# Projecting a batch's attention values in the last slots of the stage ahead, and holding them in a PSUM bank

## What is computed

```python
Q = (decoder_input @ W_q).reshape(B, Sd, HEADS, HEAD_DIM)
K = (encoder_output @ W_k).reshape(B, Se, HEADS, HEAD_DIM)
V = (encoder_output @ W_v).reshape(B, Se, HEADS, HEAD_DIM)
scores = jnp.einsum('bqhd,bkhd->bhqk', Q, K) / jnp.sqrt(jnp.float32(HEAD_DIM))
attn = jax.nn.softmax(scores, axis=-1)
out = jnp.einsum('bhqk,bkhd->bqhd', attn, V).reshape(B, Sd, E)
return out @ W_o + b_o
```

## Time and profile before

| | |
|---|---|
| median of 3 runs | 523.68 us (523.23 to 525.01) |
| the profiled execution's own time | 522.92 us |
| span in the trace | 519.5 us |
| granted TensorE clock, mean over the span | 0.963 |
| TensorE (PE) busy | 449.5 us, 87% |
| VectorE (DVE) busy | 385.5 us, 74% |
| ScalarE (ACT) busy | 291.4 us, 56% |
| GpSimd (POOL) busy | 214.4 us, 41% |

### The profile page before, as it was taken

The page is one execution under the profiler, slowest core; times in us unless marked ns, Lnnn a source line. Parts: engine busy times, 40 slices in busy tenths (PEclk is TensorE's granted clock), DMA queues, the critical chain, the costliest instruction groups (busy, mean ns, idle before and its releaser), DMA issues.

```text
span 519.5 us, 6244 instructions
## 1 busy us (share of the span) xinstructions
PE 449.5 (87%) x1923; PEld 190.0 (37%) x1923; DVE 385.5 (74%) x642; ACT 291.4 (56%) x516; POOL 214.4 (41%) x213
## 2 busy tenths in 40 slices
PE   8999779889798879899889969998979887878984
PEld 3433434224232213353342314443424332324563
DVE  5889987775779896576897896798647779732285
ACT  3244451552657753845877744646786545697434
POOL 5559795730348983421579771422000011000000
PEclk9999998999979988999999999998989989998998
DMA  6656482512695504134934213220242310000011
GB/s 217 233 152 172 114 215 78 118 37 61 182 231 138 130 1 112 26 77 132 239 96 113 63 29 84 73 72 2 63 110 62 72 52 2 2 0 1 2 40 40
DMA packets 26511, 47.31 MB, mean 91 GB/s; under 512 B 5456, under 2 KB 16368, under 8 KB 26480
## 3 DMA queue, kind: packets, MB, share of 16 engines
q1 hardware_dynamic: 24512, 44.05, 32.1%
q10 hardware_dynamic: 1968, 2.88, 2.1%
HBM read 35.19 MB, written 9.96 MB: 87 GB/s over the span
## 4 chain that ended last, share of the span: by engine, by line
PE 29%; DVE 18%; ACT 6%; issue 4%; DMA 1%; SPq 1%; ACTq 0%; POOL 0%; DVEq 0%
PE bank L665 9%; DVE MX L1615 7%; PE bank L651 6%; PE bank L726 5%; PE bank L712 4%; PE bank L703 3%; DVE W L1532 2%; ACT PT L1223 2%; PE bank L942 1%; DVE st L1498 1%; DVE OT L1625 1%; DMA x1T<-OT 1%; SPq L486 1%; PE bank L972 1%; DVE den L1621 1%
## 5 line engine op out<-in xcount | busy, mean ns | idle before, releaser
L1615 DVE TENSOR_REDUCE MX<-bank 128x1 f32<-128x512 f32 x256 | 165.9, 681 | 82.7 <-PE bank L703 78.3
L1223 ACT ACTIVATE PT<-bank 128x512 f32<-128x512 f32 x256 | 146.2, 597 | 112.9 <-PE bank L712 108.8
L703 PE MATMUL bank<-KS,QS 96*128 96x512 bf16 x240 | 91.6, 398 | 25.0 <-DVE MX L1615 24.3
L712 PE MATMUL bank<-QS,KS 99*128 99x512 bf16 x256 | 97.2, 393 | 12.3 <-ACT PT L1223 9.8
L726 PE MATMUL bank<-PT,Vs 128*32 128x512 f32 x512 | 72.6, 640 | 6.0 <-ACT PT L1223 4.3
L1917 POOL TENSOR_TENSOR W<-qT,W 128x512 f32<-128x512 f32 x48 | 63.1, 1319 | 29.0 <-DVE W L1532 17.2
L712 PEld LDWEIGHTS bank<-QS,KS 99*128 99x128 bf16 x256 | 24.2, 99 | 102.6 <-issue 59.0
L703 PEld LDWEIGHTS bank<-KS,QS 96*128 96x128 bf16 x240 | 23.7, 99 | 71.8 <-DVE MX L1615 45.5
L1948 POOL TENSOR_TENSOR MP<-MX,zero 128x16 bf16<-128x16 f32 x15 | 3.6, 240 | 107.1 <-DVE MX L1615 72.9
L1903 POOL TENSOR_TENSOR W<-kT,W 128x512 f32<-128x512 f32 x32 | 43.3, 1355 | 6.7 <-ACT kT L1074 6.7
L1532 DVE TENSOR_TENSOR_SCAN W<-bank,W 128x512 f32<-128x512 f32 x32 | 38.7, 1210 | 0.0
(11 more groups left out here) (218 smaller groups left out, 710.7 us busy)
## 6 DMA issues: line engine op xcount, KB each, us to landing
W<-v_rows SPq DMA_DIRECT2D x20, 512.0 KB, 9.2
k_parts<-parts SPq DMA_DIRECT2D x24, 128.0 KB, 2.4
KS<-k_parts SPq DMA_DIRECT2D x16, 192.0 KB, 3.7
q_parts<-parts SPq DMA_DIRECT2D x24, 128.0 KB, 2.4
QS<-q_parts SPq DMA_DIRECT2D x16, 192.0 KB, 3.6
cT<-in_cT SPq DMA_DIRECT2D x4, 512.0 KB, 3.4
xtok<-in_x SPq DMA_DIRECT2D x4, 512.0 KB, 10.1
W<-v_rows ACTq DMA_DIRECT2D x4, 512.0 KB, 5.8
```

The lines of the kernel that those rows point to most:

```text
L703: pe.matmul(bank(n, b)[:, :], QS[0:NS, h, i * P:(i + 1) * P], KS[0:NS, h, :], start=True, stop=True).then_inc(filled(n, b), 1)
L712: pe.matmul(bank(name, b)[:, :], KS[0:NR, h, kt * P:(kt + 1) * P], QS[0:NR, h, :], start=True, stop=True).then_inc(filled(name, b), 1)
L1223: act.activation(PT[:, n % 2, j, :], bank(name, b)[:, :], ACT.Exp).then_inc(emptied(name, b), 1)
L1615: dve.tensor_reduce(MX[:, NT * h + i:NT * h + i + 1], bank(n, b)[:, :], AX.X, ALU.max).then_inc(emptied(n, b), 1)
```

## The change

V1 of a batch moves to quarter (14, 1) of the stage ahead of its own and stays in bank 1 until ScalarE reads it, at the same place as before. V0 stays in its own stage for batches 1 and 2, but goes from (0, 0) to (0, 1); for the last batch it moves to (13, 1) of the stage ahead, in bank 2. To have the banks free, the maxima tiles give up bank 1 in quarters 61 to 63 of stages 0 and 1 and bank 2 from quarter 52 of stage 2 on, and mr0 is no longer in bank 1 but takes the least recently used of the maxima banks, as mr3 did already.

```diff
 SIDE_USES = {
-    (0, 0): ("V0", "b", 2), (0, 1): ("V1", "b", 1), (1, 2): ...
+    (0, 1): ("V0", "b", 2), (14, 1): ("V1", "o", 1), (1, 2): ...
...
+THIRD_USES = {**SIDE_USES, (13, 1): ("V0", "o", 2)}
+FOURTH_USES = {at: use for at, use in SIDE_USES.items() if use[0] != "V0"}
...
-    if s == 0 and (46 <= quarter <= 56 or quarter > 60) or s == 1 and (54 <= quarter <= 56 or quarter > 60):
+    if s == 0 and 46 <= quarter <= 56 or s == 1 and 54 <= quarter <= 56:
         spare.append(1)
...
-    if s == 2 and quarter >= 28 or s == 3 and (13 <= quarter <= 21 or 26 <= quarter):
+    if s == 2 and 28 <= quarter <= 51 or s == 3 and (13 <= quarter <= 21 or 26 <= quarter):
         spare.append(2)
...
 def row_bank(s, g):
-    return (1, 0, 1 if s >= 2 else 0)[g]
+    return 0 if g == 1 or s < 2 else 1
...
-                side = SIDE_USES if s else FIRST_USES
+                side = (FIRST_USES, SIDE_USES, THIRD_USES, FOURTH_USES)[min(s, 3)]
...
-                    use(f"mr{g}", stage[which], oldest(max_banks(s, NT * n + i)) if g == 3 else row_bank(s, g))
+                    use(f"mr{g}", stage[which], oldest(max_banks(s, NT * n + i)) if g in (0, 3) else row_bank(s, g))
...
                 if o is not None and b:
+                    sp.wait_ge(*full_of("V0", b))
                     sp.wait_ge(*full_of("V1", b))
                     sp.dma_start(cT[:, :, :], t["cT"][o]).then_inc(cT_in, 16)
...
-                        if b and n == 0 and i < 2:
-                            by_token(f"V{i}", b, cT, xwv, i)
+                        if b and b < LAST and (n, i) == (0, 1):
+                            by_token("V0", b, cT, xwv, 0)
+                        if o == LAST and (n, i) == (13, 1):
+                            by_token("V0", o, cT, xwv, 0)
+                        if o is not None and (n, i) == (14, 1):
+                            by_token("V1", o, cT, xwv, 1)
```

## The result

The changed kernel took 528.84 us (median of 4 runs) against 523.45 us (4 runs) before: ratio 1.0128, 95% interval 1.0075 to 1.0181. In a later session of 12 runs of it and 23 of the kernel before it came to 1.0066 (1.0021 to 1.0111). I had forecast 524.8 us, in a range of 520.8 to 527.4, and no measurable change as the likeliest outcome. The loss is 3.5 to 6.7 us.

The account below looks back on a forecast made before the run. It took VectorE to bound the ends of stages 0 and 1, TensorE the stretch after the boundary and stage 2's end. -0.4 - 1.35 + 1.4 + 1.4 (clock) = +1.05, say +1.1, giving a 524.8 us median, range 520.8 to 527.4.

Parts of the forecast that it names:

- The walk at the full clock: Tile-by-tile timing of stages 0 to 2 with fixed spacings: -0.4, -1.35 and +1.4 us.
- forecast 2.6: Ends of stages 0 and 1: m5.0 waits 2.6 us for m4.3's bank, with value row 14 behind it.
- forecast 1.4: Stage 2, both V moved and the third bank given up: 1.4 us lost on VectorE, bounds 0.3 and 2.2.
- The forecast at the full clock: Sum over stages 0, 1 and 2 before any clock loss: -0.35 us.
- I take one spell on the path out of two: Ends of stages 0 and 1: one of two possible slow-clock spells counted, turning -0.35 into +1.05 us.
- The term for the clock: Behind m5.0's wait at 1.2 GHz: value row 14 costs 0.9 more, tiles 0.5 more, 1.4 us per stage.
- a spell could reach V0: Extra to rival 1, outside the sum: V0 also at half rate, 1.7 us more each, up to 529.
- rival 1: m5.0 in (15, 1): two-bank rotation lowers the clock in both stages; +2.45 us, median 526.1; chance 0.33.
- 0.05 us: Stage 0, V1 waiting for m3.1's bank: m3.3 at 189.36 against VectorE's 189.32; cost 0.05, bounds 0 and 1.7.
- rival 3: V1 in (14, 1) queues behind bank 1's old tile, m3.3 late, mr0 and DMA delay next stage; +3 to +4; chance 0.04.
- The gain of 1.35 us at boundary 2: End of stage 1: value row 15 of the old batch at 315.4 instead of 316.77, gain 1.35 us.

Follow-up runs that it names:

- e1: The change done for batch 1's values alone (end of stage 0, start of stage 1), the rest as in the kernel before; 1.0049 of the kernel before.
- f2: The changed kernel with mr0 in the least recently used score bank instead of a maxima bank; 0.9949 of the kernel before.
- f1: The changed kernel with identity matmuls filling TensorE's waits ahead of m5.0 (stages 0 to 2) and m6.0 (stages 1 and 2); 1.0043 of the kernel before.
- h1: f1 without the filling in stage 2; 1.0041 of the kernel before.
- g3: The changed kernel run again, unaltered, in a later session; 1.0066 of the kernel before; its profile is of a slow run, 531.57 us.
- e2: The change done for batch 2's values alone (end of stage 1, start of stage 2), the rest as in the kernel before; 1.0064 of the kernel before.
- e3: The change done for batch 3's values alone (both V moved into stage 2, maxima there on two banks); 1.0052 of the kernel before.
- h2: The kernel before with identity matmuls filling its own waits, ahead of m4.0, m5.1 and V0; 0.9940 of the kernel before, median 518.52 us.
- g1: f2 with identity matmuls filling the waits ahead of m5.1 (stages 0 and 1) and m6.0 (stages 1 and 2); 0.9935 of the kernel before.

## Why the prediction was wrong

**The walk at the full clock came out nearly right, in stage 2 by luck.** V1 does fit into a gap at the end of stage 1 and in stage 0, VectorE not being idle behind it (e1: 187.94 to 189.77, then m3.3; forecast relative to the sums before it to 0.1 us). m5.0 does wait 2.5 us for m4.3's bank (forecast 2.6). Stage 2 loses 1.10 us (forecast 1.4), and the 1.5 us of VectorE's idle time behind V1 was measured as 1.45; but the forecast had made that idle time the cause, and f2 has it without the loss. The cause there is mr0 in the rotation as well. With the waits filled and no chance event, the boundaries take 31.13 (f1), 31.66 (h1) and 23.99 us: 86.78, against the 86.72 of the profile before. The forecast at the full clock was -0.35.

**The step that failed is "I take one spell on the path out of two".** The term for the clock was 1.4 us, for one value row 14 at half the rate and nothing for V0 behind it. In the profiles of the changed code (changed, g3, e1, e2) the wait is followed by a second slow spell: TensorE waits again, 0.9 to 1.4 us, for m6.0's bank, and V0 behind it takes 3.0 to 3.6 us in five of six boundaries instead of 1.9. Value row 14 takes 1.9 in four of the six. g3 against h1, which differ only in the filling and have the same chance event below, gives the price in the traces: 93.87 - 89.23 = 4.6 us of clock, 1.6 at boundary 1, where only V0 was slow, and 3.0 at boundary 2, where both were (e1 against f1: 3.1 for both). That is the prediction's own 1.4 and 1.7 added up, so the single prices were about right and their number was not. I had written that a spell could reach V0, at 1.7 us each, and had put it behind rival 1 as an extra, not in the sum. Rival 1 was the right mechanism, and its price was too small by V0. The times are less sharp: the ratios of the changed kernel (1.0128, then 1.0066) against h1's 1.0041 make the filling worth 4.6 or 1.3 us, each with an uncertainty of about 3.

**A second term was missing.** In stage 0 V1's bank is freed only just in time: I had worked out 0.05 us and no more, from one profile. When VectorE's operation ahead of m3.1 takes 2.59 us instead of 1.34, V1 waits 1.93 us instead of 0.69, and boundary 1 takes 33.58 us (h1) instead of 31.13 (f1): 2.45 us. About half of it is the longer wait; the rest is mostly the clock once more, for V1 and value row 13 behind the wait take 2.58 and 1.91 us in h1, 1.99 and 1.07 in f1. In the old layout the same event costs 1.25 (32.42 in e3, 31.17 before). So 93.87 is 86.72 + 4.64 of clock + 2.45 of this + 0.06. The event came in three of the five profiles with the changed layout of stage 0 and mr0 in the rotation (not in e1 and f1). This was rival 3's mechanism, V1 standing in the queue behind bank 1's old tile, and VectorE does then stand idle behind V1 (0.78 and 0.56 us in h1). It was not rival 3's course: mr0 and its DMA did not hold up the next stage, for TensorE waits for no transfer between 180 and 210 us in these profiles.

**The base was one profile.** The gain of 1.35 us at boundary 2 counted 1.7 us of a slow V0 that the kernel before has in some executions only (V0 there takes 1.99 us in e1's profile, 3.44 in e3's). Its runs in all sessions range from 515.8 to 529.6 us; h2 shows that the clock costs it some 3 us too. At an equal clock, and so 86.78 against 84.64, the change loses about 2 us by the wait of m5.0 in the three stages. This is worked out from traces of boundaries without the chance event. The times say more: the means of the twelve runs of h1 and of h2 are 4.5 us apart (95% interval 2.7 to 6.2), and the chance event, which comes in some runs only, may be a part of the rest. What else is in it stays open.

**The page's rule, read as rival 1 read it, came nearer.** The Trainium skill (TensorE: Matmul & The Clock Gate, section "A second HAM failure mode: psum-queue depth-cycling") reports a kernel whose clock swings between the two levels because of short idle times between groups of matmuls; it doesn't say behind which of them. The traces agree in kind: in g3 two stretches at half rate at the first boundary (V1 and V0) and two at the second (value row 14 and V0), and none there in g1, whose V0 takes 1.89 us at both. But not every such wait brought the clock down: behind the 1.96 us of m5.0's wait at g3's first boundary value row 14 took 1.06 us. The granted clock from 191 to 205 us is 0.76 in f2, whose V0 is slow, and 1.00 in g1, which is f2 with the waits filled, and in h2. f2, then h2:

```profile
191.00:205.00 14.00, 11.32 (x44) 4.41 (x48) 9.11 (x12) 4.61 (x10) 7.10 (x5) 0.76 0.38 90
```

```profile
191.00:205.00 14.00, 13.71 (x69) 5.79 (x69) 9.51 (x14) 4.38 (x9) 7.24 (x5) 1.00 0.40 105
```

## What to carry to other kernels

Moving work out of a bound stretch needs a place to hold it, and the place is paid by someone: here one small tile (mr0) that was pushed into a rotation of two banks made TensorE stand still for 2.5 us with a value row queued behind, and putting it into a score bank took the loss away in all three stages. Price a wait of TensorE by what comes after it at half the rate, up to the next long matmul on the path, and not by its length; and try filler matmuls in such waits before moving any work, since here they gave the kernel before about 3 us where the move lost 3.5 to 6.7. Take a stretch's length from several profiles, or from an unchanged stretch of the experiments, before a difference of 1 us is called a gain.

## What the runs showed of the hardware

An operation of VectorE at the end of stage 0 (two SBUF inputs, 128x512, beside two products on GpSimd) took either 1.33 to 1.35 us (11 of 16 profiles) or 2.59 to 2.60 (5 of 16), whatever was changed. In e1 GpSimd's second product is the one that is stretched, to 1.72 us; in e3 it takes 1.27 and VectorE's operation ends after it. VectorE and GpSimd of e1, then of e3:

```profile
185.35 1.34 DVE L1533 SCALAR_TENSOR_TENSOR ab<-kz,ab 128x512 f32<-128x512 f32 x1
184.88 1.26 POOL L1928 TENSOR_TENSOR W<-qT,W 128x512 f32<-128x512 f32 x1
186.10 1.72 POOL L1914 TENSOR_TENSOR W<-kT,W 128x512 f32<-128x512 f32 x1
```

```profile
185.24 2.60 DVE L1533 SCALAR_TENSOR_TENSOR ab<-kz,ab 128x512 f32<-128x512 f32 x1
184.78 1.26 POOL L1928 TENSOR_TENSOR W<-qT,W 128x512 f32<-128x512 f32 x1
186.01 1.27 POOL L1914 TENSOR_TENSOR W<-kT,W 128x512 f32<-128x512 f32 x1
```

The VectorE operation starts at nearly the same time relative to GpSimd's first product (0.47 and 0.46 us after its start). In e1 it ends 0.55 us after the end of the first product, in e3 0.56 us after the end of the second. So it looks as if either of the two could go first when the first product ends. The Trainium skill (SBUF — State Buffer, section "SBUF: two separate sides") says that a VectorE operation with two SBUF inputs and a GpSimd operation that reads SBUF use the same pair of ports, which one of them holds for its whole instruction. The traces agree with that, by these two ends, and add that the order at a handover isn't fixed. What decides it no run here shows.
